# The q and k of a head projected together, their operands laid out by transfers within SBUF, and one matmul for the row of maxima

## The reference, cut to what matters

```
x: (2, 1024, 128), 16 heads of 64, so 32 pairs of batch and head
q = (xn @ Wq) * 64 ** -0.5 ; k = xn @ Wk ; v = xn @ Wv
sim = einsum('bhid,bhjd->bhij', q, k), causal mask
attn = softmax(sim)                       # row maxima subtracted
out = attn @ v
adj = clip(attn + eye, 0, 1); deg = sum(adj)
feats = v
for l in range(2):
    feats = gelu(adj @ (feats @ gnn_w[l] + gnn_b[l]) / deg + feats)
out = out + feats @ lin_w + lin_b
return layer_norm(out @ Wo)
```

## Time and profile before

| | |
|---|---|
| median of 3 runs | 1624.57 us |
| the profiled execution | 1626.35 us, span 1624.5 us |
| granted TensorE clock, mean | 0.971 of full |
| TensorE busy | 1491.2 us (92%) |
| VectorE busy | 1286.1 us (79%) |
| ScalarE busy | 1055.2 us (65%) |
| GpSimd busy | 419.2 us (26%) |

### The profile page before, as it was taken

How to read it: one execution, slowest core, us unless ns; L and a number is a source line. 1 busy time by engine, 2 the same in 40 slices (tenths; PEclk the granted TensorE clock), 3 DMA queues, 4 the chain that set the end, 5 groups by cost and what they waited for, 6 DMA issues and landing times.

```text
span 1624.5 us, 30002 instructions
## 1 busy us (share of the span) xinstructions
PE 1491.2 (92%) x10578; PEld 1180.9 (73%) x10578; DVE 1286.1 (79%) x3374; ACT 1055.2 (65%) x2403; POOL 419.2 (26%) x544
## 2 busy tenths in 40 slices
PE   5999999999999999999999999998468999999996
PEld 4678887788778888787877887876245676667664
DVE  6588887878888888888888888865577888778875
ACT  3567676666776767767667676764345767777673
POOL 2122233222232222322232223211322432222221
PEclk9899999999999999999999999989778999999999
DMA  4000000000000000000000000000300010000100
GB/s 121 1 1 2 1 1 1 1 1 1 1 1 1 1 1 1 1 1 1 1 2 1 2 1 1 1 1 2 110 14 20 21 24 17 21 21 17 27 18 20
DMA packets 23199, 19.67 MB, mean 12 GB/s; under 512 B 8414, under 2 KB 18314, under 8 KB 23050
## 3 DMA queue, kind: packets, MB, share of 16 engines
q1 hardware_dynamic: 23050, 17.76, 4.3%
HBM read 8.84 MB, written 1.05 MB: 6 GB/s over the span
## 4 chain that ended last, share of the span: by engine, by line
PE 38%; issue 31%; DVE 14%; POOL 8%; ACT 8%; DMA 1%; SPq 0%; POOLq 0%; DVEq 0%; ACTq 0%
ACT t L1213 3%; PE PS L671 2%; PE PS L858 2%; DVE t L1554 2%; PE PS L672 2%; PE PS L706 2%; DVE t L1585 2%; PE PS L888 2%; POOL t L1350 2%; PE PS L618 2%; POOL t L1307 2%; PE PS L581 2%; POOL t L1340 2%; PE PS L619 2%; PE PS L536 1%
## 5 line engine op out<-in xcount | busy, mean ns | idle before, releaser
L1061 ACT ACTIVATE t<-PS 128x512 f32<-128x512 f32 (+3 forms) x384 | 191.2, 498 | 225.7 <-PE PS L621 138.2
L1554 DVE TENSOR_TENSOR t<-t 128x512 fp32r<-128x512 f32 (+3 forms) x384 | 246.5, 642 | 50.8 <-ACT t L1062 49.2
L1532 DVE TENSOR_REDUCE t<-PS 128x1 f32<-128x512 f32 (+3 forms) x384 | 207.8, 548 | 24.0 <-PE PS L581 23.8
L1062 ACT ACTIVATE t<-PS 128x512 fp32r<-128x512 f32 (+3 forms) x384 | 191.7, 499 | 0.0
L1350 POOL TENSOR_TENSOR t<-t 128x256 f32<-128x256 f32 x64 | 39.2, 613 | 555.3 <-DVE t L1574 555.3
L671 PE MATMUL PS<-t 128*128 128x512 f32 (+3 forms) x384 | 141.8, 370 | 21.6 <-ACT t L1095 21.6
L1415 POOL TENSOR_TENSOR t<-t 128x16 f32<-128x16 f32 x32 | 92.8, 2900 | 242.8 <-DVE t L1742 242.8
L636 PE MATMUL PS<-t 128*66 128x512 f32 (+3 forms) x384 | 137.5, 358 | 16.3 <-DVE t L1554 16.3
L1213 ACT ACTIVATE t<-PS,t 128x128 f32<-128x128 f32 x256 | 113.2, 464 | 60.1 <-DVE t L1786 60.1
L581 PE MATMUL PS<-t 128*128 128x512 f32 (+3 forms) x384 | 141.3, 378 | 3.6 <-DVE t L1532 2.7
L618 PE MATMUL PS<-t 128*128 128x512 f32 (+3 forms) x384 | 144.5, 376 | 0.1
(11 more groups left out here) (191 smaller groups left out, 4193.8 us busy)
## 6 DMA issues: line engine op xcount, KB each, us to landing
t<-t SPq DMA_DIRECT2D x60, 128.0 KB, 2.3
t<-in_L_ffn_wqkv SPq DMA_DIRECT2D x2, 768.0 KB, 7.0
t<-in_L_attn_Wv SPq DMA_DIRECT2D x2, 512.0 KB, 7.7
t<-in_c_rot SPq DMA_DIRECT2D x2, 512.0 KB, 4.7
out<-t SPq DMA_DIRECT2D x4, 256.0 KB, 2.3
t<-in_L_ffn_w SPq DMA_DIRECT2D x2, 341.0 KB
t<-in_L_attn_x SPq DMA_DIRECT2D x2, 256.0 KB, 3.3
t<-in_L_attn_Wq SPq DMA_DIRECT2D x1, 512.0 KB, 5.6
```

The costliest lines, as they stand in the source:

```text
L1061: e.activation(Es[:, k % NS, 0:n], b[:, 0:n], ACT.Exp).then_inc(a_es.up((t, k)), 1)
L1062: e.activation(Eh[:, o:o + n], b[:, 0:n], ACT.Exp).then_inc(a_eh.up((t, k)), 1)
L1532: e.tensor_reduce(n[:, c, ib:ib + 1], bank(k % 2)[:, 0:hi - lo], AX.X, ALU.max, negate=True).then_inc(d_max.up((t, k)), 1)
L1554: e.tensor_tensor(El[:, o:o + n], Es[:, k % NS, 0:n], f32(Eh[:, o:o + n]), ALU.subtract).then_inc(d_el.up((t, k)), 1)
```

## The change

k and q of a head are projected together: the weights stand side by side (k in columns 0 to 63, q in 64 to 127), so that one group of three matmuls per half gives k in partitions 0 to 63 and q in 64 to 127. A column qsc (1 and 0.125) scales both in one copy. ScalarE writes the high parts to K1, VectorE the low parts to Q1. Then SyncE moves them: part copies q's high part to Q2 and k's low part to K2, and double writes k's high part over q's in K1 and q's high part over k's low one in Q1. A second transfer waits for the first two. The maxima are no longer split: one float32 matmul with the identity gives them as 8 rows of 128, ScalarE copies these to MR, and a transfer lays them out as one row 64 of Q2.

```diff
-        WD = [sb1([P, 2, 2, P], F32R) for _ in range(2)]
+        WD = [sb1([P, 2, P], F32R) for _ in range(2)]
+        MR = sb1([8, P], F32R)
+        qsc = sb1([P, 1])
...
+        def apart(t, c):
+            return s_apart[c], 32 * (t + 1)
+        def twice(t, c):
+            return s_twice[c], 32 * (t + 1)
+        def row_ready(t):
+            return s_row, 16 * (t + 1)
...
+            def part(t):
+                r = t % RB
+                for c in range(2):
+                    sl = slice(c * 512, (c + 1) * 512)
+                    q.wait_ge(*a_hi[t, c])
+                    e.dma_start(f32(Q2[r][0:64, sl]), f32(K1[r][64:128, sl])).then_inc(s_apart[c], 16)
+                    q.wait_ge(*d_low[t, c])
+                    e.dma_start(f32(K2[r][0:64, sl]), f32(Q1[r][0:64, sl])).then_inc(s_apart[c], 16)
+            def double(t):
+                r = t % RB
+                for c in range(2):
+                    sl = slice(c * 512, (c + 1) * 512)
+                    q.wait_ge(*apart(t, c))
+                    e.dma_start(f32(K1[r][64:128, sl]), f32(K1[r][0:64, sl])).then_inc(s_twice[c], 16)
+                    e.dma_start(f32(Q1[r][0:64, sl]), f32(Q2[r][0:64, sl])).then_inc(s_twice[c], 16)
+            def mrow(t):
+                q.wait_ge(*a_row[t])
+                e.dma_start(f32(Q2[t % RB][64:65, :]).rearrange("a (k p) -> a k p", k=8), f32(MR[:])).then_inc(s_row, 16)
+            part(0)
+            double(0)
+            for t in range(NH):
+                if t + 1 < NH:
+                    part(t + 1)
+                mrow(t)
+                if t + 1 < NH:
+                    double(t + 1)
...
@@ TensorE, proj @@
-                elif which == "q":
-                    q.wait_ge(*a_eh[t - 2, 10 + c])
-                else:
-                    q.wait_ge(*d_max[t - 1, 10 + c])
+                elif t:
+                    q.wait_ge(*a_eh[t - 2, 10 + c])
@@ TensorE, smax and scores @@
-                q.wait_ge(*d_low[t, "q", 1])
-                q.wait_ge(*a_hi[t, "k", 1])
+                q.wait_ge(*twice(t, 0))
+                q.wait_ge(*twice(t, 1))
...
-                q.wait_ge(*a_row[t, 1])
-                q.wait_ge(*w_q2[t, 1])
+                q.wait_ge(*row_ready(t))
@@ TensorE, mrow @@
-                for k in range(4):
-                    m = e.matmul(bank(4)[0:66, k * P:(k + 1) * P], NM[:, 4 * c + k, :], identR[:], start=True, stop=True)
-                m.then_inc(p_row.up((t, c)), 1)
+                e.matmul(bank(4)[0:8, 0:P], nm[t % 2][:, 0, :], identF[:], start=True, stop=True).then_inc(p_row.up(t), 1)
@@ ScalarE @@
-                e.activation(T1[:, c * 512:(c + 1) * 512], bank(b), ACT.Copy, scale=sc).then_inc(a_hi.up((t, which, c)), 1)
+                e.activation(K1[t % RB][:, c * 512:(c + 1) * 512], bank(b), ACT.Copy, scale=qsc[:, 0:1]).then_inc(a_hi.up((t, c)), 1)
-                e.copy(Q2[t % RB][64:66, c * 512:(c + 1) * 512], bank(4)[64:66, :]).then_inc(a_row.up((t, c)), 1)
+                e.copy(MR[:], bank(4)[0:8, 0:P]).then_inc(a_row.up(t), 1)
@@ VectorE, lower @@
-                if which == "k":
-                    m = e.tensor_tensor(K2[r][0:64, sl], bank(b)[0:64, :], f32(K1[r][0:64, sl]), ALU.subtract)
-                else:
-                    m = e.scalar_tensor_tensor(Q1[r][64:128, sl], bank(b)[64:128, :], 0.125, f32(Q1[r][64:128, sl]),
-                                               ALU.mult, ALU.subtract)
+                e.scalar_tensor_tensor(Q1[r][:, sl], bank(b), qsc[:, 0:1], f32(K1[r][:, sl]), ALU.mult,
+                                       ALU.subtract).then_inc(d_low.up((t, c)), 1)
@@ VectorE, the last step of smax @@
-                e.tensor_tensor(n[:, 0, 4:8], n[:, 0, 4:8], n[:, 1, 4:8], ALU.min).then_inc(own.up(), 1)
-                q.wait_ge(*own.now())
-                e.tensor_copy(NM[:, :, 64], n[:, 0, :]).then_inc(own.up(), 1)
-                q.wait_ge(*own.now())
-                e.tensor_tensor(NM[:, :, 65], n[:, 0, :], f32(NM[:, :, 64]), ALU.subtract).then_inc(d_nm.up(t), 1)
+                e.tensor_tensor(n[:, 0, 4:8], n[:, 0, 4:8], n[:, 1, 4:8], ALU.min).then_inc(d_nm.up(t), 1)
@@ GpSimd @@
-                e.tensor_copy(Q2[t % RB][0:64, sl], f32(Q1[t % RB][0:64, sl])).then_inc(w_q2.up((t, c)), 1)
...
@@ TensorE, before the main loop @@
-            proj(0, "q", 0, 2)
-            proj(0, "k", 0, 3)
-            proj(0, "q", 1, 4)
-            proj(0, "k", 1, 5)
+            for c in range(2):
+                proj(0, c, 2 + c)
+            for c in range(2):
+                proj(1, c, 4 + c)
+            for c in range(2):
+                projv(0, c)
             for k in range(NTL):
                 smax(0, k)
-                if k in (1, 3):
-                    projv(0, k // 2)
-                if k in (5, 6, 7, 8):
-                    proj(1, ("q", "k")[k % 2], (k - 5) // 2, k - 3)
@@ VectorE, end of an iteration @@
                 feats(t, 0)
-                lower(t + 2, "q", 0, 2)
-                lower(t + 2, "q", 1, 3)
+                lower(t + 2, 0, 2)
+                lower(t + 2, 1, 3)
                 share(t, 0)
-                lower(t + 2, "k", 0, 0)
                 graph1(t, 1)
-                lower(t + 2, "k", 1, 1)
                 feats(t, 1)
```

More of the change, by code:

```diff
@@ L247, in program @@
         p_lin = signal("p_lin", range(6))
-        p_proj = signal("p_proj", projs)
+        p_proj = signal("p_proj", halves)
         p_pv = signal("p_pv", halves)
         p_max = signal("p_max", maxes)
-        p_row = signal("p_row", halves)
+        p_row = signal("p_row", heads)
         p_sc = signal("p_sc", by_tile)
@@ L262, in program @@
         a_lin = signal("a_lin", range(1, 5))
-        a_hi = signal("a_hi", projs)
+        a_hi = signal("a_hi", halves)
         a_v = signal("a_v", halves)
-        a_row = signal("a_row", halves)
+        a_row = signal("a_row", heads)
         a_es = signal("a_es", by_tile)
@@ L277, in program @@
         d_turn = signal("d_turn", range(4))
-        d_low = signal("d_low", projs)
+        d_low = signal("d_low", halves)
         d_vl = signal("d_vl", halves)
@@ L301, in program @@
         w_wr = signal("w_wr", heads)
-        w_q2 = signal("w_q2", halves)
         w_n2 = signal("w_n2", halves)
@@ L352, in program @@
         s_vs = [sem(f"vs{i}") for i in range(4)]
+        s_apart = [sem(f"s_apart{c}") for c in range(2)]
+        s_twice = [sem(f"s_twice{c}") for c in range(2)]
+        s_row = sem("s_row")
         ld = {n: sem("l_" + n) for n in ("xa", "xb", "xc", "id", "wq", "wk", "gin", "wv", "w0", "wv2", "cm", "wg", "ww1",
@@ L584, in smax, with mrow @@
                 m.then_inc(p_max.up((t, k)), 1)
-            def mrow(t, c):
+            def mrow(t):
                 if t >= NH:
@@ L666, in graph2 @@
                 if k == 0:
-                    q.wait_ge(*(d_p1[t - 1] if t else d_low[1, "q", 1]))
+                    q.wait_ge(*(d_p1[t - 1] if t else d_low[1, 1]))
                 if k == 4:
@@ L785, in tensor @@
                 av(t, 7)
-                proj(t + 2, "q", 0, 2)
+                proj(t + 2, 0, 2)
                 av(t, 8)
+                proj(t + 2, 1, 3)
                 av(t, 10)
                 av(t, 11)
-                proj(t + 2, "q", 1, 3)
-                proj(t + 2, "k", 0, 0)
-                mrow(t + 1, 0)
+                graph2(t, 0)
+                mrow(t + 1)
                 graph1(t, 1)
-                proj(t + 2, "k", 1, 1)
-                graph2(t, 0)
                 graph2(t, 2)
-                mrow(t + 1, 1)
                 graph2(t, 1)
@@ L1113, in scalar @@
             values()
-            proj(0, "q", 0, 2)
-            proj(0, "k", 0, 3)
-            proj(0, "q", 1, 4)
-            proj(0, "k", 1, 5)
-            for k in range(NTL):
-                if k in (1, 3):
-                    projv(0, k // 2)
-                if k in (5, 6, 7, 8):
-                    proj(1, ("q", "k")[k % 2], (k - 5) // 2, k - 3)
-            mrow(0, 0)
-            mrow(0, 1)
+            for c in range(2):
+                proj(0, c, 2 + c)
+            for c in range(2):
+                proj(1, c, 4 + c)
+            for c in range(2):
+                projv(0, c)
+            mrow(0)
             for t in range(NH + 2):
@@ L1318, in widen @@
                 if t >= 2:
-                    q.wait_ge(*p_proj[t - 2, "q" if t == 3 else "k", 1])
+                    q.wait_ge(*p_proj[t - 2, 1])
                 for i in range(2):
@@ L1668, in vector @@
             e.tensor_copy(cmB[:], cm[:]).then_inc(d_ident.up("cm"), 1)
-            lower(0, "q", 0, 2)
-            lower(0, "k", 0, 3)
-            lower(0, "q", 1, 4)
-            lower(0, "k", 1, 5)
+            for c in range(2):
+                lower(0, c, 2 + c)
+            for c in range(2):
+                lower(1, c, 4 + c)
+            for c in range(2):
+                projv(0, c)
             for k in range(NTL):
                 smax(0, k)
-                if k in (1, 3):
```

(3 more changed lines are left out.)

108 lines of the change are left out of this document (37 added, 71 removed).

## The result

The changed kernel takes **1668.68 us** (median of 4 runs, 1666.52 to 1673.60) against 1625.30 (4 runs, 1624.45 to 1627.21) before: a ratio of 1.0261, 95% interval 1.0242 to 1.0281. That is 43.4 us slower, where the forecast was 19.4 slower. The profiled execution took 1667.36 us, span 1665.6, against 1626.35 and 1624.5: +41.0, and it is this difference that the rows divide.

What follows compares the result with a forecast made beforehand. TensorE's queue was taken to bound the kernel before, the transfer chain to set the changed kernel's period. Profiled 1626.35 with +12, +8 and -0.3 gave 1646; against the median 1644 us, range 1614 to 1712.

Steps and rivals of the forecast that it cites:

- the start, +8: Start: two rounds of transfers before smax(0), at 30.8; smax(1) at 43.5 to 45 instead of 36.22; +8 us.
- the transfers in the thirty boundaries: Heads 2 to 31: smax waits for the transfer chain, +0.4 us a head, +12 us, ends -12 and +90.
- Premise: First part is a TensorE queue; what leaves it is worth its pitch, as long as nothing else comes late.
- TensorE's net of -1.71 us: TensorE, per head: 1.45 us of projections and 0.48 of maxima matmuls leave, one f32 matmul of 0.22 comes.
- Step 1: TensorE at iteration end: graph2(t,0) waits for feats, a new gap of 0.7 to 0.8 us replacing the 0.38.
- Step 2: ScalarE's copies of the halves, second at 610.85 to 611.45; VectorE's lower, 0.69 each, ends at 612.65 and 613.35.
- step 3: SyncE's issues: row of maxima at 614.3, doublings from 614.85, the last at 616.65, landing 618.95.
- Step 4: TensorE done at 617.15, smax waits until 619.0 to 619.1; idle gap about 1.9 us, head 0.4 us longer.
- Rival A: Clock falls at the new gap before smax; at half of thirty boundaries, 3 us each, +45: 1689 us; chance 0.36.
- B: Transfer chain hidden, smax at 618.0 or before, 0.67 us a head gained; 1607 to 1613, so 1610; chance 0.12.
- C: It balances: chain before smax ends 0.2 us early, -6, against +5 to +8 at the start; 1624; chance 0.10.
- What would show it: Profile signs: period 33.8 us, 1.9 idle before smax, 0.7 before graph2(0), landings 2.2 to 2.3, VectorE busy down some 45.

Runs made afterwards that it cites:

- one round: Changed kernel with high parts written to a staging tile, three transfers per half from there, GpSimd copying k, lower on 64 partitions again; 1634.22 us, ratio 1.0052.
- the experiment with two queues: Changed kernel with q's copies from K1 to Q2 issued by ScalarE, leaving SyncE seven transfers a head instead of nine; 1653.03 us, ratio 1.0165.
- the version with k's low parts later: Against one round and late loads: VectorE's two subtractions for k's low parts put behind graph1(t,1); 1598.90 us, ratio 0.9819.
- the row of maxima last: Changed kernel with SyncE issuing the doublings of head t+1 ahead of the row of maxima of head t; 1653.23 us, ratio 1.0166.
- the loads moved: Changed kernel with the start's last three loads issued behind the first transfers of heads 0 and 1; 1661.52 us, ratio 1.0219.
- one round and late loads: One round with the start's last three loads issued behind the transfers of heads 0 and 1; 1630.75 us, ratio 1.0017.

## Why the prediction was wrong

The direction, the mechanism and the place of each wait in a head were right; the size was under half. The sum gave 1646 for the profiled execution and 1667.36 came, 21.4 more. **Three terms of the sum failed**: the start, +8, measured 15.8; the transfers in the thirty boundaries, all taken at medians, +12, measured 18; and late transfers with a fall of the clock behind them, which the sum put at nothing, measured 10.3. The last head took 4.2 less than said, because it lost a fall of the clock that it had before; that is luck. Against the steps, in order:

- *Premise: what leaves TensorE's queue is worth its pitch.* About right for the kernel before (0.66 of 0.94), not for what is left once the transfers are hidden: one round has TensorE's whole saving in it and gave 0.03 us a head, until VectorE's order was changed.
- *TensorE's net of -1.71 us.* From graph1(t,0) to the last graph2 matmul, waits taken off, it was 618.67 - 603.30 - 1.06 = 14.31 us before and 549.41 + 0.23 - 535.56 - 1.26 = 12.82 after: -1.49. The small matmul took 0.32 instead of 0.22, and the first matmul behind each wait takes 0.34 to the next one where it took 0.23 in a row.
- *Step 1, a new gap of 0.7 to 0.8 before graph2(t,0)*: 0.58, released by VectorE, and the 0.38 gone. Right.
- *Step 2, lower ends at 612.65 and 613.35, and step 3, the issues*: the issues of part and of the row come within 0.2 of what was said. The last doubling was forecast 13.35 us behind graph1(t,0) (616.65 - 603.30) and went at 549.07 - 535.56 = 13.51. Right within 0.2; the row's issue took 0.68 where room for 0.55 stood.
- *Step 4, smax at 619.0 to 619.1*, 15.75 behind graph1(t,0): measured 15.98, the 0.16 of the issue and some of the landing, 2.4 for the last doubling where 2.3 stood. The idle time was 1.74, forecast 1.9. Behind smax 0.06 more. The term "+0.4 a head, +12" was mis-sized: **0.68 a head, +20**. That 0.3 missed by 8 us, since thirty boundaries carry it, less the 2 of the eight heads that were slow before.
- *The start, +8*: smax(0) at 32.17 for 30.8, smax(1) at 48.10 for 43.5 to 45, which is 11.9 late and not 8. And I followed the start to smax(1) and stopped there, as if the head behind it took what it took before. It took 84.06 - 48.10 = 36.0 us, before 68.28 - 36.22 = 32.1: TensorE came out of two waits of 8.11 and 5.42 us with its clock at half and kept it until 77.0, and the experiment with two queues, with the same smax(1) and the clock back 9 us sooner, took 31.9. Moving the loads gave 8.0 of the 15.8 back, 4.1 of them by the loads themselves; one round of transfers, with the row of maxima behind them, 5.0 more; 2.8 stayed. The prediction also had it that widen is never waited for; in the start TensorE waits 1.27 for it once, at 19.78.
- *Late transfers, put at nothing*: the steps took every issue and landing at its median and kept the late ones for the upper bound. Four heads of thirty had one, as the second part of the kernel before has (landings up to 4.1, one issue of L455 of 1.80), and were 10.3 us longer with the falls.
- *Rival A, the clock falls at the new gap*: both more and less true than drawn. In 26 heads, with a wait of 1.7 us and in four of them 1.9 to 2.0, it didn't fall. It fell in four with 2.3 to 3.15, for 1.4 to 1.7 us each rather than 3, and these waits were themselves a late transfer. Filling them gave no time back that can be told from the spread of the runs. Its sign, a clock below 0.97 over the span, was there, 0.959; but of the 21 us of full clock missing against before, 15 lie in the start, where no rival had put them.
- *Rivals B and C* did not happen. B, the chain hidden, is what one round of transfers made of it; with its own added work on VectorE and GpSimd it brought about 1631, not 1610.
- *What would show it*: VectorE's busy time fell by 46.0 (forecast 45). TensorE's fell by 29.6 and not by more, since a matmul of 512 columns that is 0.39 long at full clock is 0.63 long at half (before, at 59.50 and 49.80), and the start has more of these. The period was 34.1 and not 33.8; the new gap (0.58), the wait before smax (1.74) and the landings (2.3 to 2.4) were near what was said.

What stays open: why single issues on SyncE take 1.4 to 2.0 us instead of 0.6 (1.61 at 125.03; 1.42 in the start, at 19.88; 2.00 once in the version with k's low parts later), and what the kernel before does with all of the third that it kept of TensorE's 0.94 us (0.28 a head, of which the longer wait for El is 0.22). Why the clock's lower level ends at 68 us in one version and at 77 in another, with the same waits in front, and whether the start's last 2.8 us are the clock, is open too. The falls in the four heads rest on one profiled execution.

## What to carry to other kernels

When engine work is replaced by transfers within SBUF, count the issues on the queue before the bytes: here two dependent rounds of four, with one more between them, cost 5 us of issue beside two landings of 2.4, and a staging tile that makes all of them depend on one producer hid them. Once the added wait is gone, look at the waits that took its place, and through them at the order of VectorE's and ScalarE's programs: a subtraction moved behind work that others wait for was worth 32 us, where TensorE's shorter program alone had brought none. And follow a delay at the start to the first steady head, with the clock in view.

## What the runs showed of the hardware

- In the changed kernel TensorE's clock fell behind waits of 2.30 to 3.15 us in full work, and in none of the 26 heads with 1.7 to 2.0. That is no rule: with the row of maxima last it didn't fall behind 2.28 (at 748.25), with the loads moved it fell once behind 1.72 (919.00), and in the version with one round and late loads in three heads with no wait over 0.9 (0.90, 0.32 and 0.68 within 5 us; clock 0.72 from 111 to 117). The Trainium skill ("TensorE: Matmul & The Clock Gate", Why this matters for your kernels) would see no drop behind idle gaps of 2.75 us and less; the rows don't agree, and the measurement decides. At the start the lower level held for 51.2 us while TensorE was busy 36.4 of them, 28.2 of the last 28.9.
- A transfer of 128 KB between partitions took 2.3 to 2.4 us to land at the median of each line, 2.2 at the least, up to 3.3 in the doublings and up to 8.6 in the start, behind the loads. Its issue costs the queue 0.46 when the queue was idle and mostly 0.60 when the transfers follow each other.
- Times of the versions with transfers spread wider than the kernel before's (one round with late loads 1622.31 to 1640.56, the version with two queues only 1652.57 to 1653.41). Their profiled executions differ in the number of late transfers and falls of the clock (none in the thirty heads of the version with two queues), which would account for it; that is not shown.
